# One MLP block and one KAN block per round of a common loop in a mixture-of-experts kernel

## What is computed

```
x = x + 0.5 * moe(layernorm(x))
x = x + attention_and_ffn(layernorm(x))
x = x + 0.5 * moe(layernorm(x))
moe: each row goes to the 2 best of 8 experts by x @ gate_W, weighted by softmax
  experts 0..3 (MLP): gelu(x @ W1 + b1) @ W2 + b2                       128 -> 512 -> 128
  experts 4..7 (KAN): z = basis(layernorm(x)*g0+c0) @ W0 + b0            128*8 -> 256
                      y = basis(layernorm(z)*g1+c1) @ W1 + b1            256*8 -> 128
  basis(h): 1 - tanh((h - grid) / 2)^2 at 8 grid points, from sigmoids here: s*(s-1)*(-4)
```

## Time and profile before

| | us |
|---|---|
| median of 3 runs | 728.19 |
| lowest, highest | 725.35, 728.44 |
| the profiled execution | 732.84 |
| its span, first to last instruction | 731.0 |

### The profile page before, as it was taken

The page is one execution under the profiler, slowest core; times in us unless marked ns, Lnnn a source line. Parts: engine busy times, 40 slices in busy tenths (PEclk is TensorE's granted clock), DMA queues, the critical chain, the costliest instruction groups (busy, mean ns, idle before and its releaser), DMA issues. The chain is left out here.

```text
span 731.0 us, 18200 instructions
## 1 busy us (share of the span) xinstructions
PE 577.0 (79%) x6003; PEld 470.5 (64%) x6004; DVE 455.7 (62%) x1172; ACT 274.2 (38%) x766; POOL 251.5 (34%) x314
## 2 busy tenths in 40 slices
...
GB/s 268 346 279 88 92 96 22 14 22 14 14 15 17 44 84 3 3 13 4 12 5 4 3 0 1 36 342 367 66 50 50 23 15 14 18 18 14 14 12 176
DMA packets 41679, 48.94 MB, mean 67 GB/s; under 512 B 7328, under 2 KB 33280, under 8 KB 40352
## 3 DMA queue, kind: packets, MB, share of 16 engines
...
## 5 line engine op out<-in xcount | busy, mean ns | idle before, releaser
L981 ACT ACTIVATE k_sig<-k_h1T 128x256 f32<-128x256 f32 x264 | 84.5, 402 | 144.7 <-DVE k_h1T L872 144.7
L774 PEld LDWEIGHTS k_y_ps<-kan_w,k_basis 128*128 128x128 f32 x1056 | 127.3, 198 | 7.2 <-issue 5.6
L774 PE MATMUL k_y_ps<-kan_w,k_basis 128*128 x1056 | 127.8, 281 | 5.1 <-DVE k_basis L847 5.1
L764 PE MATMUL k_z_ps<-kan_w,k_basis 128*128 x528 | 126.3, 394 | 0.0
L764 PEld LDWEIGHTS k_z_ps<-kan_w,k_basis 128*128 128x128 f32 x528 | 100.6, 195 | 16.9 <-issue 0.8
L847 DVE SCALAR_TENSOR_TENSOR k_basis<-k_sig 128x512 f32<-128x512 f32 x132 | 85.6, 690 | 10.6 <-ACT k_sig L981 10.6
L640 POOL DMA_INDIRECT y_rows<-k_y,k_rows_out x33 | 42.2, 1280 | 106.2 <-DVE k_y L879 100.3
L974 ACT ACTIVATE k_sig<-k_h0T 128x128 f32<-128x128 f32 x264 | 55.8, 294 | 3.3 <-DVE k_h0T L835 3.3
L898 DVE TENSOR_TENSOR m_z<-m_z_ps,mlp_b 128x512 f32<-128x512 f32 x40 | 27.7, 692 | 42.8 <-PE m_z_ps L743 42.8
L1457 DVE TENSOR_REDUCE p_minus_max<-p_ps 128x6 f32<-128x960 f32 (+1 forms) x44 | 46.0, 1118 | 6.8 <-PE p_ps L1374 5.3
L1493 ACT ACTIVATE got<-p_ps 128x960 f32<-128x960 f32 (+1 forms) x44 | 39.2, 944 | 27.5 <-PE p_ps L1409 27.5
...
...
## 6 DMA issues: line engine op xcount, KB each, us to landing
...
```

Source lines behind the costliest of these rows:

```text
L764: last = nc.tensor.matmul(z_ps, basis0[:, g], k.kan_w0[:, bass.ds(e, 1), g], start=(g == 0), stop=(g == G - 1))
L774: last = nc.tensor.matmul(y_ps, basis1[:, g, c], k.kan_w1[:, bass.ds(e, 1), c, g], start=(g == 0 and c == 0), stop=(g == G - 1 and c == F2 ...
L981: ins = nc.scalar.activation(sig1[:, g], h1T[:], ACT.Sigmoid, bias=float(-GRID[g]))
```

## The change

`moe_blocks` gets three loops instead of two. The first runs MLP blocks alone, two per iteration, `pairs` times. The second, `Fori(0, joint)`, runs one KAN round and one MLP block per iteration. The third, `Fori(0, alone)`, runs KAN rounds alone. Two MLP blocks run in the filling part between the first and the second loop, and one in the tail. With n MLP blocks (at least 9) and m KAN blocks (at least 5), the counts are

```diff
-NS = MAXB + 7
+NS = MAXB + 9
 assert NS % 2 == 0
 LEAD = 4
+LEAST_MLP, LEAST_KAN = 9, 5
...
-    q.dma_start(k.mlp_b1[:], a.mlp_b1.partition_broadcast(P)).then_inc(k.mlp_loaded[n], 16)
...
+                nc.vector.tensor_scalar(n_mlp[:], blocks_up_to[:, E2 - 1:E2], float(LEAST_MLP), None, ALU.max)
...
-                link(nc.vector.tensor_copy(k.n_mlp[:], blocks_up_to[:, E2 - 1:E2]))
-                nc.vector.tensor_scalar(kan_rows[:], k.slot_no[:], blocks_up_to[:, E2 - 1:E2], float(T),
-                                        ALU.is_ge, ALU.mult)
-                mlp_blocks = dve.value_load(k.n_mlp[0:1, 0:1], min_val=0, max_val=MAXB)
+                nc.vector.tensor_copy(k.n_rounds[:, 3:4], n_mlp[:])
+                nc.vector.tensor_scalar(n_kan[:], blocks_up_to[:, NE - 1:NE], float(LEAST_KAN), -2.0, ALU.max, ALU.add)
+                link(nc.vector.tensor_scalar(room[:], n_mlp[:], -7.0, None, ALU.add))
+                nc.vector.tensor_scalar(kan_rows[:], k.slot_no[:], n_mlp[:], float(T), ALU.is_ge, ALU.mult)
+                link(nc.vector.scalar_tensor_tensor(both[:], n_kan[:], -1.0, room[:], ALU.add, ALU.min))
+                link(nc.vector.scalar_tensor_tensor(both[:], both[:], -1.0, n_mlp[:], ALU.mult, ALU.add))
+                link(nc.vector.tensor_scalar(pairs_i[:], both[:], -2.0, None, ALU.add))
+                link(nc.vector.tensor_scalar(k.n_rounds[:, 0:1], pairs_i[:], 1, None, ALU.logical_shift_right))
+                link(nc.vector.tensor_copy(half_f[:], k.n_rounds[:, 0:1]))
+                link(nc.vector.scalar_tensor_tensor(in_pairs[:], half_f[:], -2.0, n_mlp[:], ALU.mult, ALU.add))
+                nc.vector.tensor_scalar(k.n_rounds[:, 1:2], in_pairs[:], -3.0, None, ALU.add)
+                link(nc.vector.scalar_tensor_tensor(half_f[:], in_pairs[:], -1.0, n_kan[:], ALU.mult, ALU.add))
+                link(nc.vector.tensor_scalar(k.n_rounds[:, 2:3], half_f[:], 3.0, None, ALU.add))
+                mlp_blocks = nc.values_load_multi_w_load_instructions(
+                    k.n_rounds[0:1, :], engines=[dve.engine], min_val=1, max_val=NS,
+                    skip_runtime_bounds_check_because=BOUND)[1][3]
                 at_first = nc.s_assert_within(mlp_blocks + 2, 0, NQ - 3, skip_runtime_bounds_check_because=BOUND)
+                nc.vector.tensor_tensor(tmp[:], pick[:], bc(prob[:], 1, TOPK), ALU.mult)
+                link(nc.vector.reciprocal(den[:], den[:]))
+                nc.vector.tensor_reduce(k.weight[:], tmp[:], AX.X, ALU.add)
+                link(nc.vector.tensor_scalar(den[:], den[:], 0.5, None, ALU.mult))
+                nc.vector.tensor_tensor(k.weight[:], k.weight[:], bc(den[:], 1, TOPK), ALU.mult)
...
+                if n == 0:
+                    pe.wait_ge(k.b1_loaded, 16)
+                    nc.tensor.transpose(b1_ps[:], b1_rows_sb[:], k.ident[0:E2 * FC, 0:E2 * FC]).then_inc(b1_turned, 1)
...
+                def m_scatter(j, u):
+                    pool.wait_ge(m_rows_ready, j)
+                    pool.wait_ge(m_y_ready, j + 1)
+                    pool.sem_inc(noted, 1)
+                    put_rows(m_y[u], m_rows[u][:, 1:2], m_stored[u])
...
+                def k_round(r, scatter_mlp):
+                    pool.wait_ge(loaded, r * 16 + 64)
+                    k_take_rows(r)
+                    k_scatter(r)
+                    scatter_mlp()
+                    pool.wait_ge(turned, r + 4)
+                    pool.sem_inc(noted, 1)
+                    get_rows(x_in, k_rows[:, 0:1], loaded)
+                    power(r + 2)
+                    k_scattered(r)
...
+                with pool.Fori(0, joint) as r:
+                    j = r + 2 * pairs + 3
+                    near = within(j + 2, 3, NQ)
+                    nc.gpsimd.tensor_copy(j_rows[:], k.rows_of[:, bass.ds(near, 3)].rearrange("p q w -> p (q w)")
+                                          ).then_inc(j_rows_ready, 1)
+                    pool.wait_ge(m_turned, j + 1)
+                    pool.wait_ge(j_rows_ready, r + 1)
+                    pool.sem_inc(noted, 1)
+                    get_rows(j_x_in, j_rows[:, 0:1], j_loaded)
+
+                    def j_scatter():
+                        pool.wait_ge(m_y_ready, j + 1)
+                        pool.sem_inc(noted, 1)
+                        put_rows(j_y, j_rows[:, 5:6], j_stored)
+
+                    k_round(r, j_scatter)
+                    pool.wait_ge(j_loaded, r * 16 + 16)
+                    pool.wait_ge(j_stored, r * 16 + 16)
+                    pool.sem_inc(j_y_free, 1)
+
+                with pool.Fori(0, alone) as i:
+                    k_round(i + joint, nothing)
...
+                def by_w1(j):
+                    pe.wait_ge(m_w1_ready, j)
+                    pe.wait_ge(m_xT_ready, j)
+                    for c in range(FC):
+                        last = nc.tensor.matmul(m_z_ps[:, c], m_w1[:, c * P:(c + 1) * P], m_xT[:],
+                                                start=True, stop=True)
+                    last.then_inc(m_z_done, 1)
...
+                def m_step(j, u, nth, e):
+
+                    pe.wait_ge(m_z_ready, j)
+                    by_w1(j + 1)
+                    m_turn(m_x_in[u], m_loaded[u], nth)
+                    by_w2(j, e)
...
-                        for c in range(FC):
-                            last = nc.tensor.transpose(m_zT_ps[:, c], m_z[:, c * P:(c + 1) * P], k.ident[:])
-                        last.then_inc(m_zT_done, 1)
-                        by_w1(i + 1, e_pair[u + 2])
...
                 by_w0(0, e_first[0])
-                by_w2(2 * pairs, mlp_experts(pe, 2 * pairs, 1)[0])
+                m_step(2 * pairs + 1, 0, pairs + 2, e_fill[0])
                 turn_zn(0)
                 pe.wait_ge(h0_ready, 2)
                 turn(2)
                 by_w0(1, e_first[1])
-                with pe.Fori(0, rounds) as i:
-                    e_last, _, e_next, _ = kan_experts(pe, i + 1, 4)
-                    by_kan_w1(i, e_last)
-                    turn_zn(i + 1)
-                    pe.wait_ge(h0_ready, i + 3)
-                    turn(i + 3)
-                    by_w0(i + 2, e_next)
+                m_step(2 * pairs + 2, 1, pairs + 2, e_fill[1])
...
+                def k_round(r, fill):
+                    e_last, _, e_next, _ = kan_experts(pe, r + 1, 4)
+                    by_kan_w1(r, e_last)
+                    fill()
+                    turn_zn(r + 1)
+                    pe.wait_ge(h0_ready, r + 3)
+                    turn(r + 3)
+                    by_w0(r + 2, e_next)
...
+                with pe.Fori(0, joint) as r:
+                    j = r + 2 * pairs + 3
+                    e = mlp_experts(pe, j, 1)[0]
+
+                    k_round(r, lambda: by_w2(j, e))
+                    pe.wait_ge(m_z_ready, j)
+                    by_w1(j + 1)
+                    m_turn(j_x_in, j_loaded, r + 1)
+                with pe.Fori(0, alone) as i:
+                    k_round(i + joint, nothing)
...
+                by_w2(j_last, e_mlp)
...
+                def m_take_z(j, e):
+
+                    dve.wait_ge(m_z_done, j)
+                    bias = k.mlp_b1[:, bass.ds(e, 1)].rearrange("p o c -> p (o c)")
+                    if j is not first:
+                        dve.wait_ge(m_hT_ready, j - 1)
+                    nc.vector.tensor_tensor(m_z[:], m_z_ps, bc(bias, 2, P), ALU.add).then_inc(m_z_ready, 1)
...
+                def k_round(r, after_y, after_stats):
+                    e_last, e, e_next, e_ahead = kan_experts(dve, r + 1, 4)
+                    take_y(r, e_last)
+                    after_y()
+                    affine1(r + 1, e)
+                    dve.wait_ge(sig0_done, H0 * r + 3 * H0)
+                    affine0(r + 3, e_ahead)
                     for h in range(H1 - 1):
-                        hills1(i + 1, h)
-                    take_z(i + 2, e_next)
-                    hills1(i + 1, H1 - 1)
-                    z_stats(i + 2)
-                    hills0(i + 3, 0)
-                e_before, e_last, e, _ = kan_experts(dve, rounds, 4)
-                normalize_z(rounds)
-                hills0(rounds + 1, 1)
-                affine1(rounds, e_last)
-                take_y(rounds - 1, e_before)
-                for h in range(H1 - 1):
-                    hills1(rounds, h)
-                take_z(rounds + 1, e)
-                hills1(rounds, H1 - 1)
-                z_stats(rounds + 1)
-                normalize_z(rounds + 1)
+                        hills1(r + 1, h)
+                    take_z(r + 2, e_next)
+                    hills1(r + 1, H1 - 1)
+                    z_stats(r + 2)
+                    after_stats()
+                    hills0(r + 3, 0)
+                    normalize_z(r + 2)
+                    hills0(r + 3, 1)
...
+                with dve.Fori(0, joint) as r:
+                    j = r + 2 * pairs + 3
+                    e_mlp, e_after = mlp_experts(dve, j, 2)
+
+                    def j_take_y():
```

(58 more changed lines are left out.)

378 lines of the change are left out of this document (200 added, 178 removed).

## The result

The changed kernel takes 683.61 us (median of 4 runs, 681.72 to 684.14) against 728.32 us before, a ratio of 0.938 [0.934, 0.942]. Its profiled execution took 683.25 us with a span of 681.4 us. The forecast was 687, the range 675 to 709.

The account below looks back on a forecast made before the run. Both loops stand at TensorE's work or a little above, with bubbles to win. First MoE -18.4, second -17.9, tail -3, ahead of the landing -2: -41.3 us, giving 687 us on the median's scale; range 675 to 709.

Parts of the forecast that it names:

- The counts and the sum: Both MoEs: 11 and 13 joint rounds, 4 and 1 KAN rounds alone; all terms together -41.3 us.
- The joint round: Joint loop, TensorE: 9.67 us of its own work as floor, 10.0 us taken, ceiling 10.9 us.
- no stall for zn: Joint loop, TensorE: the wait for normalized z before the transposes vanishes, since W2 stands between; 0.36 us in a KAN round.
- The nearest second: ScalarE in a joint round: 8.3 us of work, 9.3 us with a loop head, under TensorE's 10.0 us.
- The price of a table switch: ScalarE in the joint loop: each of two table loads costs 1.28 us, with the next activation at once behind it.
- rival 2: Joint loop and filling part: table switches cost twice their row and ScalarE becomes the bound; 740 us, chance 0.07.
- VectorE and GpSimd: Joint round: VectorE busy 7.5 us, GpSimd one more gather and scatter of 1 us each; together they cost nothing.
- A round alone: KAN-only loop: between 7.56 and 7.92 us, 7.75 taken, since the power waits for the variance only.
- Landing to first y: Each MoE, first gathered rows to first KAN y: 17 us of start plus 14 of filling, 31 us, against 68.1 and 71.1.
- Tail: End of both MoEs: W2 falls into the wait for the last sigmoids, less idle may keep the clock; -3 us together.
- Ahead of the landing: Before each MoE's first rows: b1's broadcast goes, VectorE count work is added; between +1 and -3.8 us, -1 each taken.

Follow-up runs that it names:

- The moved W2: Control edited: in the joint loop W2 goes behind z and GpSimd's scatter of its result behind the power; 703.57 us.
- the old order: Control edited: VectorE's order of the kernel before put into the new loops, with normalize first and take_y after affine1; 685.09 us.
- the second control: Repeat of the control, the changed kernel with its four loop counts loaded into registers one by one; 685.41 us.

## Why the prediction was right, point by point

*The counts and the sum.* 11 and 13 joint rounds, 4 and 1 alone: right. The mechanism, that two loops standing at TensorE's work with bubbles become one without, is what the run with one joint round and the run with W1 twice show. The medians moved by -44.7 us where -41.3 was forecast. In the spans the miss is -8.3 us, and its terms don't all point one way: joint rounds -14.6, rounds alone +0.4, landing to first y +0.7, tails +4.5, ahead of the landings and the end +0.7.

*The joint round: forecast 10.0, floor 9.67; measured 9.25.* What was off is a size. y was counted at its row's 3.76 us and takes 3.57 us from start to start; each transpose or turn was counted at 0.15 us and takes 0.11; W2 takes 0.90 us for 0.98. That is 0.42 us under the floor. Part of it is the neighbour: y's row is 3.76 us where y stands directly behind z (before, and at 186.34 and 648.87 after), and 3.65 behind the turn; in the same way W1, now behind z, has a row of 1.08 us where W2 behind y has 0.97. The rest is that the next group's loads start before the row ends. A KAN round with nothing to wait for is 7.25 us (179.09 to 186.34), not 7.56. Nor was the round of 7.92 us in the earlier trace rows a usual one: nine of that loop's fifteen took 8.10 or 8.11 us. And the 0.33 us put on top for a wait was for nothing. It would have made 24 x 0.75 = 18 us; 3.4 come back in the first joint round of each MoE (10.23 and 11.26 us, with TensorE's issue late by 0.95 and 1.98 us) and in one round of 9.46 and 9.48 in each.

*Why there is no stall for zn.* The prediction had W2 hide it. The moved W2 shows that W1 and the turn, which stand ahead of y, are enough, with zn 1.3 us ahead of its transposes in a round that has no idle time (152.33, 153.60). A step with two covers was credited to one of them.

*ScalarE*: forecast 8.3 us busy, measured 7.9. "The nearest second" was right, but its 9.3 us against 10.0 weren't the way to measure the distance: the circle through W2 had 0.6 us left. The price of a table switch, 1.28 us with nothing after it, holds at every load shown here, and in the run with 48 more of them. The Trainium skill, page "ScalarE: Activation LUTs", section "What ACT_TABLE_LOAD costs", adds a drain of about 1380 ns to every switch; no trace of this case shows it, neither ahead of a load nor behind one, and rival 2 with it is out.

*VectorE and GpSimd*: forecast 7.5 us for VectorE, measured 7.3 (81.67 / 103 of 9.25). "Cost nothing" holds in the joint loop.

*A round alone: forecast 7.75; measured 7.25, 7.89, 8.42, 8.35.* Wrong. The prediction listed what the power no longer waits for, and not that VectorE's loop head and take_y had moved in between zn and h1T, nor that the power, now earlier, runs beside VectorE's hills: there it takes 1.00 us, and 0.57 where it doesn't (152.69 in a joint round). How the cost divides between the two is not shown: with the old order a steady round was 0.2 us shorter, and the power was no shorter. The three later rounds together cost 1.4 us more than forecast, the first ones of the two MoEs 0.5 us less each, so only 0.4 us in all.

*Landing to first y: 31; measured 31.1 and 31.5.* Its two halves are 17.65 (forecast 17) and 13.45 (14). The filling part, TensorE's loads of the changed kernel:

```profile
62.71 0.14 PEld L829 LDWEIGHTS k_xT_ps<-ident,k_x_in 128*128 128x128 f32 x1
63.66 3.32 PEld L835 LDWEIGHTS k_z_ps<-kan_w,k_basis 128*128 128x128 f32 x16 [0.81 <-issue]
...
70.48 0.20 PEld L852 LDWEIGHTS k_znT_ps<-ident,k_zn 128*128 128x128 f32 x2 [1.40 <-DVE k_zn L960]
...
70.76 3.32 PEld L835 LDWEIGHTS k_z_ps<-kan_w,k_basis 128*128 128x128 f32 x16
```

Against the earlier trace rows: the idle time of 3.67 us is 1.40, and z takes 3.32 us instead of 5.79, at a granted clock of 1.00 instead of 0.56. The MLP steps were forecast at 2.2 us and take 2.63 (W1 at 58.19, then at 60.82), for the wait on W1's copy; the loop head and the start were a little cheaper.

*Tail: forecast -3; measured +2.1 and -0.6.* Wrong. The last y of both kernels stands behind the last sigmoids, and these came later by VectorE's loop head, take_y and the hills of a padding block; the run with the old order gave 0.95 and 0.60 us of it back. The other half, that less idle time would keep the clock, fell too: the idle time did not shrink. ('s 6.51 us were read as half clock; the granted clock over them is 0.54, and 0.69 over the 5.19 us of the first MoE.) The last y of the first MoE in the changed kernel, TensorE's loads:

```profile
219.73 5.28 PEld L845 LDWEIGHTS k_y_ps<-kan_w,k_basis 128*128 128x128 f32 x32 [3.05 <-issue]
```

The last y of the first and of the second MoE in the second control:

```profile
222.08 5.28 PEld L842 LDWEIGHTS k_y_ps<-kan_w,k_basis 128*128 128x128 f32 x32 [2.69 <-issue]
...
661.38 3.65 PEld L842 LDWEIGHTS k_y_ps<-kan_w,k_basis 128*128 128x128 f32 x32 [2.68 <-issue]
```

*Ahead of the landing: forecast -1 in each MoE; measured -1.2 and +0.5.* Wrong, and the first number is luck. GpSimd's first gather before:

```profile
40.48 1.20 POOL L457 DMA_INDIRECT m_x_in<-x_rows,rows_of  x1 [23.29 <-DVE k_rows_first L393]
```

and after:

```profile
40.66 1.20 POOL L477 DMA_INDIRECT m_x_in<-x_rows,rows_of  x1 [23.50 <-DVE k_rows_first L420]
```

With the broadcast or without, it waits for VectorE, and it starts 0.18 us later, not earlier. The 1.2 us lie between gather and turn, 5.75 us before and 4.40 after, and in the twelve traces without the broadcast this way takes anything from 4.40 to 6.54 us. In the new form the broadcast put back does delay this gather, by 0.9 us; in the kernel before it did not hold it. In the second MoE the gather waited for the rows' DMA before and waits for VectorE now, and nothing was won: from the last y's end to this gather it is 256.15 us before and 256.54 after. In place of the 3.83 us of the earlier trace rows, SyncE's queue stands 2.90 us at b2's broadcast. The wait for found_ps, 4.33 us before, still had 0.91 us left: the added steps fitted under it.
